# The shared-key attention stage of a two-layer decoder: float32 matmuls as three products of float32r high and low parts, and weight loads placed in other stages

## The chip, the cores and the metric

The kernel runs on one core of a Trainium2 chip. The metric is the device time of one execution in microseconds, as the median over runs. The core has TensorE (PE, matmuls, writes PSUM only), VectorE (DVE), ScalarE (ACT), GpSimd (POOL, no access to PSUM) and SyncE (SP, which here only issues DMAs). Each engine works through its own instruction stream in order and waits for the others by semaphores.

## The reference

The reference is a decoder of two layers on x of 2 batches x 512 tokens x 256 channels, each layer a mixer, a cross attention over 1,024 context rows, and a block of experts. The part that the change touches is the mixer of the second layer, an attention whose eight query heads share one key and one value projection:

```python
def _L1_attn_ref(x, proj_q, proj_k, proj_v, proj_o):
    Q = jnp.einsum('bnd,hdk->bhnk', x, proj_q)
    K = jnp.einsum('bmd,dk->bmk', x, proj_k)
    V = jnp.einsum('bmd,dv->bmv', x, proj_v)
    logits = jnp.einsum('bhnk,bmk->bhnm', Q, K)
    weights = jax.nn.softmax(logits, axis=-1)
    O = jnp.einsum('bhnm,bmv->bhnv', weights, V)
    Y = jnp.einsum('bhnv,hdv->bnd', O, proj_o)
    return Y
x = x + _L1_attn_ref(_layernorm(x, axis=-1), ...)
```

Heads have 128 columns. Behind this mixer come a cross attention that picks, for each query, the best context row ("hard cross"), and the second block of experts (256 to 1,024 channels, eight experts).

## The kernel before, in words

The program runs six stages one after the other: `mamba_stage`, `cross_stage`, `experts0_stage`, `shared_kv_stage`, `hard_cross_stage`, `experts1_stage`. Each is a block in which every engine has its own instruction list, and the engines meet between blocks.

**The stage of the change, `shared_kv_stage` (from line 1768).** A unit is one head of one batch: 16 units, batch by batch. Inside, one pipeline step (a "round" g) belongs to a tile of 128 queries, so a unit is four rounds, and there are 64 tiles. The stage has this course:
- Start: PE runs five bf16 products without use (L121), transposes the normalised input into PSUM (L112, 16 transposes), ACT copies that to `XT` (L1317). PE makes K (L1938) and V (L1947), ACT and DVE copy them out (L1901, L1847), and PE waits for these copies and for the weights `wq` and `wo`.
- The loop on PE, in this order in each round g = 4n + qt: `scores(g)` (L1970, 128 x 512); in rounds with qt 0 or 1 half of the next unit's `query_part` (L1959); `transposes(g - 3)`, four of 128 x 128 (L1978); one of four products of `output` (unit n - 1 where qt is 3, else unit n - 2) (L1988); one of four of `project` (unit n - 3) (L2000, 256 columns). Two PSUM banks each serve scores and transposes by turns.
- The other engines in a round: DVE takes the maximum of each row of scores (L1854), negates it (L1856), and makes the inverse of the sum of the round before (L1863); ACT makes the exponential with its sum (L1922); POOL multiplies by the inverse sum (L1835), 1.57 us each; DVE copies the transposes to `PT` (L1870); ACT copies the queries (L1907) and the output (L1913), each once per unit.
- DVE's order in a round: first the copy of the transposes g - 4, then the maximum of g, then the inverse sum of g - 1.
- `output(n, 0)`, the first output product of unit n, waits until all four sets of transposes of the unit are copied, which is in round 4n + 7.
- End: DVE adds the result to `X` (L1878) and `FirstQueries` (L2093, L2099) begins the next stage's queries.

**Weights.** SP loads `wq` and `wo` (1 MB each) at the start of this stage, and behind them the eight weight blocks of the second experts (L170, 1 MB each) into `area`, a buffer of 16,384 words per partition that the first experts' weights had used. `wk` and `wv` are loaded in the first experts' stage. The second experts' PE waits for all eight (`weights.loaded`).

**The hard cross stage.** It has eight units. SP's list waits for the end of an earlier unit, loads the constant rows (`tails`) and copies the query rows of unit u in parts (L2185, 64 KB each), four units ahead at most.

Of the kernel before, what the change touches and what calls it, by code (L numbers as in the profile page):

```python
# [8 lines left out]
F32 = mybir.dt.float32  # L9
BF16 = mybir.dt.bfloat16  # L10
# [4 lines left out]
P = 128  # L15
B, S, D = 2, 512, 256
T = B * S
# [1750 lines left out]
def shared_kv_stage(nc, ctx, sh, A):  # L1768
# [25 lines left out]
    def sem(name):  # L1794
# [3 lines left out]
    nm = Norm(nc, ctx, sh, "s_n")  # L1798
    nm.xn_loaded = sh.xn_back
    following = NextStatistics(sh, sem)  # L1800
    wq, wo = sb("wq", [P, H, KD, DK]), sb("wo", [P, H, D])
    wk, wv = sh.wk, sh.wv
    KTr, V = sb("KT", [P, T]), sb("V", [P, NT, DK])
    QT = [sb(f"QT{n}", [P, S]) for n in range(2)]
# [7 lines left out]
    wq_in, wo_in = sem("wq_in"), sem("wo_in")  # L1812
    kv_mm, k_ready, v_ready = sem("kv_mm"), sem("k_ready"), sem("v_ready")
    q_mm, q_ready = sem("q_mm"), sem("q_ready")
    s_mm, mx_ready, nmx_ready, p_ready, rs_ready, pn_ready, t_mm, pt_ready = (
        sem(n) for n in ("s_mm", "mx_ready", "nmx_ready", "p_ready", "rs_ready", "pn_ready", "t_mm", "pt_ready"))
    o_mm, o_ready, y_mm, y_taken = sem("o_mm"), sem("o_ready"), sem("y_mm"), sem("y_taken")

    with stage, nc.Block() as block:

        @block.sync
        def _(sp):
            sp.dma_start(wq[:, :, :, :], A["s_wq"]).then_inc(wq_in, 16)
            sp.dma_start(wo[:, :, :], A["s_wo"]).then_inc(wo_in, 16)
            queries.load(sp)
            for e in range(ExpertWeights.EXP):
                sh.weights[1].load_expert(sp, e)

        @block.gpsimd
        def _(pool):  # L1830
            for g in range(G):
# [10 lines left out]
        def _(dve):  # L1842
            for b in range(B):
                for i in range(0, TB, 2):
                    n = B + (b * TB + i) // 2
                    dve.wait_ge(kv_mm, n + 1)
                    dve.tensor_copy(V[:, b * TB + i:b * TB + i + 2, :],  # L1847
                                    PS[:, 4 + n % 4, 0:2 * DK].rearrange("p (i c) -> p i c", i=2)).then_inc(v_ready, 1)
# [16 lines left out]
            def take_transposes(g):  # L1865
                n, qt = divmod(g, TB)
                dve.wait_ge(t_mm, g + 1)
                if n >= 2:
                    dve.wait_ge(o_mm, n - 1)
                dve.tensor_copy(PT[n % 2][:, :, qt * P:(qt + 1) * P],  # L1870
                                PS[:, 2 + g % 2, :].rearrange("p (m q) -> p m q", m=TB)).then_inc(pt_ready, 1)
# [21 lines left out]
            queries.vector(dve, following.rstd_ready, nm.xT_done)  # L1893
# [3 lines left out]
        def _(act):  # L1897
            nm.scalar(act)
            for b in range(B):
                act.wait_ge(kv_mm, b + 1)  # L1900
                act.activation(KTr[:, b * S:(b + 1) * S], PS[:, 4 + b, :], ACT.Copy).then_inc(k_ready, 1)  # L1901

            def take_q(n):
                act.wait_ge(q_mm, n + 1)
                if n >= 2:
                    act.wait_ge(s_mm, (n - 1) * TB)
                act.activation(QT[n % 2][:, :], PS[:, 4, :], ACT.Copy).then_inc(q_ready, 1)  # L1907

            def take_o(n):
# [3 lines left out]
                act.activation(OT[n % 2][:, :], PS[:, 5, :], ACT.Copy).then_inc(o_ready, 1)  # L1913
# [18 lines left out]
        def _(pe):  # L1932
            spare_matmuls(pe, sh, 7, 5)
            nm.tensor(pe)
            for b in range(B):
                pe.wait_ge(nm.xT_ready, KD * (b + 1))
                for k in range(KD):
                    last = pe.matmul(PS[:, 4 + b, :], wk[:, k, :], XT[:, k, b * S:(b + 1) * S],  # L1938
                                     start=(k == 0), stop=(k == KD - 1))
                last.then_inc(kv_mm, 1)  # L1940
            for i in range(0, NT, 2):
                n = B + i // 2
                if n >= 4:
                    pe.wait_ge(k_ready, n - 3)
                for j in range(2):
                    for k in range(KD):
                        last = pe.matmul(PS[:, 4 + n % 4, j * DK:(j + 1) * DK], XT[:, k, (i + j) * P:(i + j + 1) * P],  # L1947
                                         wv[:, k, :], start=(k == 0), stop=(k == KD - 1))
                last.then_inc(kv_mm, 1)
            pe.wait_ge(k_ready, B)  # L1950
            pe.wait_ge(v_ready, NT // 2)
            pe.wait_ge(wq_in, 16)
            pe.wait_ge(wo_in, 16)

            def query_part(n, k):
                b, h = divmod(n, H)
                if n >= 1 and k == 0:
                    pe.wait_ge(q_ready, n)
                last = pe.matmul(PS[:, 4, :], wq[:, h, k, :], XT[:, k, b * S:(b + 1) * S],  # L1959
                                 start=(k == 0), stop=(k == KD - 1))  # L1960
# [3 lines left out]
            def scores(g):  # L1964
# [5 lines left out]
                pe.matmul(PS[:, g % 2, :], QT[n % 2][:, qt * P:(qt + 1) * P], KTr[:, b * S:(b + 1) * S],  # L1970
# [1414 lines left out]
```

## Time and profile before

| | us |
|---|---|
| median of 3 runs | 1010.96 |
| lowest, highest | 1007.08, 1012.14 |
| span of the profiled execution (first to last instruction) | 1003.7 |
| first experts' stage, from about 390 | to 498.5 |
| shared-key stage, start to first query | 498.5 to 509.2 |
| its loop | 509.2 to 704.9 |
| hard cross stage | 711.4 to 881 |
| second experts' stage | 881 to the end |

The profiled execution is one more execution than the three timed ones; no time beside its span is given for it, so it has to be set against the median. In the profile, PE is a matmul, PEld a weight load beside it. A record such as "560.83 1.02 PE L1970 MATMUL ... x2" is two matmul records of line 1970 that start at 560.83 us; ends of matmuls are modelled and overlap the next start, so that the time that PE spends is read from start to start. A float32 matmul has two records. "[0.99 <-PE PS L1970]" is idle time of the engine ahead of the instruction and what ended it. PEclk is the granted clock of PE as a share of 2.4 GHz.

### The profile page before, as it was taken

Reading aid. Unit: us, or ns where it says so; the run is one execution under the profiler, and the core shown is the slowest. Engines: PE = TensorE matmul, PEld = TensorE weight load, DVE = VectorE, ACT = ScalarE, POOL = GpSimd, SP = SyncE. Lnnn points to the kernel's source line nnn. Section 1 sums busy time; section 2 is a strip of 40 time slices with the busy share of each in tenths; the row PEclk is TensorE's granted clock in tenths of the full one; section 3 lists DMA queues with packets and bytes.
Section 4 is the critical chain, followed back from the end, with each engine's and each line's share of the span. In section 5 each row is a group of like instructions: output and inputs, shape, how many; then the busy total and the mean of one; then the engine's idle time right before and its main releaser. Section 6 shows DMA issues by size and latency. Waiting matters only on the chain. (4 is left out here: it accounts for less than half of the span.)

```text
span 1003.7 us, 12848 instructions
## 1 busy us (share of the span) xinstructions
PE 915.3 (91%) x4110; PEld 459.1 (46%) x4110; DVE 642.4 (64%) x1323; ACT 468.3 (47%) x928; POOL 322.9 (32%) x328
## 2 busy tenths in 40 slices
PE   5889879999999986799999999999988999859996
PEld 2445545333323235366755555555432332534565
DVE  5866558888899823455245555655689897444654
ACT  3886444677777771112133333332216777342321
POOL 7326646200000000166235545554230000115923
PEclk9999998999999997799899999999998999969999
DMA  5040036022223803633491000000200010066200
GB/s 154 1 157 0 1 61 107 1 50 49 49 50 96 289 1 112 242 105 116 144 394 40 1 0 1 1 1 1 65 17 2 32 33 1 1 246 200 75 17 27
DMA packets 41654, 73.79 MB, mean 74 GB/s; under 512 B 8964, under 2 KB 27780, under 8 KB 40436
## 3 DMA queue, kind: packets, MB, share of 16 engines
q1 hardware_dynamic: 36372, 59.68, 19.4%
q0 software_dynamic: 4400, 13.11, 4.1%
q8 instruction: 35, 0.57, 0.2%
q10 hardware_dynamic: 816, 0.17, 0.1%
q14 instruction: 31, 0.25, 0.1%
HBM read 49.67 MB, written 10.49 MB: 60 GB/s over the span
## 5 line engine op out<-in xcount | busy, mean ns | idle before, releaser
L1080 DVE TENSOR_REDUCE c_amx<-PS 128x1 f32<-128x512 f32 x256 | 159.1, 682 | 27.4 <-PE PS L980 27.1
L1173 ACT ACTIVATE c_aE<-PS 128x512 f32<-128x512 f32 x256 | 132.5, 602 | 47.1 <-PE PS L992 46.9
L1835 POOL TENSOR_SCALAR s_Pn<-s_Pr,s_rs 128x512 f32<-128x512 f32 x64 | 100.1, 1566 | 101.5 <-DVE s_rs L1863 101.2
L71 POOL TENSOR_SCALAR rstd<-mv 128x4 f32<-128x4 f32 x8 | 1.9, 233 | 335.5 <-DVE mv L94 335.5
L980 PE MATMUL PS<-c_aKs,c_aQs 99*128 99x512 bf16 x256 | 96.4, 387 | 5.1 <-DMA c_aQs<-area 3.6
L1922 ACT ACTIVATE s_Pr<-PS,s_nmx 128x512 f32<-128x512 f32 x64 | 44.0, 688 | 116.2 <-DVE s_nmx L1856 116.2
L992 PE MATMUL PS<-c_aQs,c_aKs 99*128 99x512 bf16 x256 | 94.5, 380 | 3.5 <-ACT c_aE L1173 2.3
L1854 DVE TENSOR_REDUCE s_mx<-PS 128x1 f32<-128x512 f32 x64 | 44.3, 691 | 68.7 <-PE PS L1970 68.7
L1080 DVE TENSOR_REDUCE h_amx<-PS 128x1 f32<-128x512 f32 x128 | 79.6, 682 | 8.8 <-PE PS L980 8.5
L1173 ACT ACTIVATE h_aE<-PS 128x512 f32<-128x512 f32 x128 | 67.7, 600 | 21.8 <-PE PS L992 21.4
L1003 PE MATMUL PS<-c_aE,c_VB 128*17 128x512 f32 x512 | 67.4, 598 | 0.1
L1970 PE MATMUL PS<-s_KT,s_QT 128*128 128x512 f32 x128 | 65.6, 594 | 1.0 <-ACT s_QT L1907 0.7
L1988 PE MATMUL PS<-s_PT,s_V 128*128 128x512 f32 x128 | 65.7, 595 | 0.3 <-ACT s_OT L1913 0.3
L980 PEld LDWEIGHTS PS<-c_aKs,c_aQs 99*128 99x128 bf16 x256 | 24.9, 98 | 79.0 <-DVE c_amx L1080 55.4
L3179 PE MATMUL PS<-area,g_XsT 128*128 x120 | 56.7, 617 | 0.5 <-ACT g_XsT L3116 0.5
L980 PE MATMUL PS<-h_aKs,h_aQs 99*128 99x512 bf16 x128 | 49.8, 397 | 7.7 <-DVE h_amx L1080 7.1
L1870 DVE COPY s_PT<-PS 128x512 f32<-128x512 f32 x64 | 44.2, 690 | 10.9 <-PE PS L1978 10.9
L992 PE MATMUL PS<-h_aQs,h_aKs 99*128 99x512 bf16 x128 | 48.7, 392 | 2.1 <-ACT h_aE L1173 1.2
L1978 PEld LDWEIGHTS PS<-ident,s_Pn 128*128 128x128 f32 x256 | 31.9, 141 | 32.5 <-issue 26.1
L3121 ACT ACTIVATE g_H<-g_H 128x1024 f32<-128x1024 f32 x15 | 15.9, 1058 | 53.0 <-DVE g_H L3055 53.0
L992 PEld LDWEIGHTS PS<-c_aQs,c_aKs 99*128 99x128 bf16 x256 | 24.6, 98 | 32.2 <-ACT c_aE L1173 9.6
L1978 PE MATMUL PS<-ident,s_Pn 128*128 128x128 f32 x256 | 38.4, 273 | 0.0
(440 smaller groups left out, 1696.8 us busy)
## 6 DMA issues: line engine op xcount, KB each, us to landing
area<-in_e_w SPq DMA_DIRECT2D x16, 512.0 KB, 9.5
area<-in_g_w SPq DMA_DIRECT2D x8, 1024.0 KB, 17.1
c_aKs<-area SPq DMA_DIRECT2D x48, 128.0 KB
g_B<-in_g_b SPq DMA_DIRECT2D x1, 4096.0 KB, 14.3
c_aQs<-area SPq DMA_DIRECT2D x48, 64.0 KB
h_aQs<-h_QP SPq DMA_DIRECT2D x48, 64.0 KB
early<-in_ctxT SPq DMA_DIRECT2D x2, 1024.0 KB, 8.6
e_B<-in_e_b SPq DMA_DIRECT2D x1, 2048.0 KB
```

What stands on the lines that cost most here:

```text
L980: pe.matmul(PS[:, n % MB, :], self.Qs[u % self.NQ][:, j, qt * P:(qt + 1) * P], self.Ks[self.key_buffer(u)][:, j % self.KH, half * BANK:(ha ...
L992: pe.matmul(PS[:, MB + n % XB, :], self.Ks[self.key_buffer(u)][:, j % self.KH, kt * P:(kt + 1) * P], self.Qs[u % self.NQ][:, j, :], start= ...
L1003: last = pe.matmul(PS[32 * j:32 * j + VW, 6, :], self.V[:, self.value_unit(u), kt, j % self.KH, :], self.E[kt % 2][:, j, :], start=(kt == ...
L1080: dve.tensor_reduce(self.mx[:, qt, j, half:half + 1], PS[:, n % MB, :], AX.X, ALU.max).then_inc(self.max_done, 1)
L1173: act.activation(self.E[kt % 2][:, j, :], PS[:, MB + x % XB, :], ACT.Exp, scale=0.25).then_inc(self.exp_done, 1)
L1835: pool.tensor_scalar(Pn[g % NPB][:, :], Pr[g % NPB][:, :], rs[:, g % NPB:g % NPB + 1], None, ALU.mult).then_inc(pn_ready, 1)
L1854: dve.tensor_reduce(mx[:, g % NPB:g % NPB + 1], PS[:, g % 2, :], AX.X, ALU.max).then_inc(mx_ready, 1)
L1870: dve.tensor_copy(PT[n % 2][:, :, qt * P:(qt + 1) * P], PS[:, 2 + g % 2, :].rearrange("p (m q) -> p m q", m=TB)).then_inc(pt_ready, 1)
L1970: pe.matmul(PS[:, g % 2, :], QT[n % 2][:, qt * P:(qt + 1) * P], KTr[:, b * S:(b + 1) * S], start=True, stop=True).then_inc(s_mm, 1)
L1978: last = pe.transpose(PS[:, 2 + g % 2, m * P:(m + 1) * P], Pn[g % NPB][:, m * P:(m + 1) * P], sh.ident[:, :])
L1988: last = pe.matmul(PS[:, 5, :], V[:, n // H * TB + m, :], PT[n % 2][:, m, :], start=(m == 0), stop=(m == TB - 1))
L3179: last = pe.matmul(PS[:, 1 + p % 2 * NB1 + half, :], XsT[p % 2][:, k, :], W1[:, k, bass.ds(e * F + half * BANK, BANK)], start=(k == 0), st ...
```

## The change

Each operand of the stage's matmuls is split into a high part, which is the value written as float32r, and a low part, the value less the high part, also written as float32r. Each product f x m becomes f_high x m_high + f_high x m_low + f_low x m_high, accumulated in PSUM. Transposes stay as they are. High parts are written by ACT (for `wk`, `wv`, `wo` by DVE), low parts by DVE (for `wq` by POOL). The copy of the transposes moves from DVE to ACT, and each low part is a new DVE instruction, in the rounds as the diff shows. The tiles `PT` and the split `wq` and `wo` take all of `area`; so `wq` and `wo` are loaded in the first experts' stage, into buffers of their own, and the second experts' weights in the hard cross stage, two behind the query rows of each of the units 4 to 7.

The diff, without the declarations of semaphores and the comments of context:

```diff
@@ shared_kv_stage
-    PT = [sb(f"PT{n}", [P, TB, S]) for n in range(2)]
-    OT = [sb(f"OT{n}", [P, S]) for n in range(2)]
+    PT = [[overlaid(f"PT{part}{n}", [P, TB, S]) for part in "hl"] for n in range(2)]
+    wqs, wos = ([overlaid(f"{name}{part}", shape) for part in "hl"]
+                for name, shape in (("wq", [P, H, KD, DK]), ("wo", [P, H, D])))
+    XTs, KTs, Vs = split("XT", [P, KD, T]), split("KT", [P, T]), split("V", [P, NT, DK])
+    wks, wvs = split("wk", [P, KD, DK]), split("wv", [P, KD, DK])
+    QT, OT = ([split(f"{name}{n}", [P, S]) for n in range(2)] for name in ("QT", "OT"))
...
         def _(sp):
-            sp.dma_start(wq[:, :, :, :], A["s_wq"]).then_inc(wq_in, 16)
-            sp.dma_start(wo[:, :, :], A["s_wo"]).then_inc(wo_in, 16)
             queries.load(sp)
-            for e in range(ExpertWeights.EXP):
-                sh.weights[1].load_expert(sp, e)
...
         def _(pool):
+            pool.wait_ge(wqh_ready, 1)
+            pool.tensor_tensor(wqs[1][:, :, :, :], wq[:, :, :, :], wqs[0][:, :, :, :].bitcast(F32),
+                               ALU.subtract).then_inc(wq_ready, 1)
...
         def _(dve):
+            for w, parts in ((wk, wks), (wv, wvs)):
+                dve.tensor_copy(parts[0][:, :, :], w[:, :, :]).then_inc(wh_ready, 1)
+            dve.tensor_copy(wos[0][:, :, :], wo[:, :, :]).then_inc(wh_ready, 1)
+            dve.wait_ge(wh_ready, 2)
+            for w, parts in ((wk, wks), (wv, wvs)):
+                dve.tensor_tensor(parts[1][:, :, :], w[:, :, :], parts[0][:, :, :].bitcast(F32),
+                                  ALU.subtract).then_inc(w_ready, 1)
+            dve.wait_ge(wh_ready, 3)
+            dve.tensor_tensor(wos[1][:, :, :], wo[:, :, :], wos[0][:, :, :].bitcast(F32),
+                              ALU.subtract).then_inc(w_ready, 1)
+            for g in range(KD * B):
+                b, k = divmod(g, KD)
+                cols = slice(b * S, (b + 1) * S)
+                dve.wait_ge(xkvh_ready, g + 1)
+                dve.tensor_tensor(XTs[1][:, k, cols], PS[:, g, :], XTs[0][:, k, cols].bitcast(F32),
+                                  ALU.subtract).then_inc(xkv_ready, 1)
+            for n in range(NKV):
+                high, low = kv_parts(n)
+                dve.wait_ge(xkvh_ready, KD * B + n + 1)
+                dve.tensor_tensor(low, kv_bank(n), high.bitcast(F32), ALU.subtract).then_inc(xkv_ready, 1)
...
+            def low_queries(n):
+                dve.wait_ge(qh_ready, n + 1)
+                dve.tensor_tensor(QT[n % 2][1][:, :], PS[:, 4, :], QT[n % 2][0][:, :].bitcast(F32),
+                                  ALU.subtract).then_inc(q_ready, 1)
+
+            def low_output(n):
+                dve.wait_ge(oh_ready, n + 1)
+                dve.tensor_tensor(OT[n % 2][1][:, :], PS[:, 5, :], OT[n % 2][0][:, :].bitcast(F32),
+                                  ALU.subtract).then_inc(o_ready, 1)
...
+                dve.wait_ge(pth_ready, g + 1)
+                dve.tensor_tensor(PT[n % 2][1][:, :, cols], PS[:, 2 + g % 2, :].rearrange("p (m q) -> p m q", m=TB),
+                                  PT[n % 2][0][:, :, cols].bitcast(F32), ALU.subtract).then_inc(pt_ready, 1)
...
-            for g in range(G + LAG + 1):
-                if g > LAG:
-                    take_transposes(g - LAG - 1)
+            low_queries(0)
+            for g in range(STEPS):
+                n, qt = divmod(g, TB)
+                v, m = output_part(g - 1)
+                if 0 <= v < UN and m == TB - 1:
+                    low_output(v)
                 if g < G:
                     maximum(g)
                 if 1 <= g <= G:
                     inverse_sum(g - 1)
+                if 0 <= g - LAG - 1 < G:
+                    low_transposes(g - LAG - 1)
+                if qt == 2 and n + 1 < UN:
+                    low_queries(n + 1)
...
         def _(act):
-            nm.scalar(act)
+            act.activation(wqs[0][:, :, :, :], wq[:, :, :, :], ACT.Copy).then_inc(wqh_ready, 1)
+            for g in range(KD * B):
+                b, k = divmod(g, KD)
+                act.wait_ge(xT_done, g + 1)
+                act.activation(XTs[0][:, k, b * S:(b + 1) * S], PS[:, g, :], ACT.Copy).then_inc(xkvh_ready, 1)
+            for n in range(NKV):
+                act.wait_ge(kv_mm, n + 1)
+                act.activation(kv_parts(n)[0], kv_bank(n), ACT.Copy).then_inc(xkvh_ready, 1)
...
             for g in range(STEPS):
                 n, qt = divmod(g, TB)
+                if 0 <= g - LAG - 1 < G:
+                    take_transposes(g - LAG - 1)
...
         def _(pe):
+            def products(out, fixed, moving, start, stop):
+                for i, (f, m) in enumerate(((0, 0), (0, 1), (1, 0))):
+                    last = pe.matmul(out, fixed[f], moving[m], start=(start and i == 0), stop=(stop and i == 2),
+                                     skip_group_check=True)
+                return last
...
+            pe.wait_ge(w_ready, 2)
             for b in range(B):
-                pe.wait_ge(nm.xT_ready, KD * (b + 1))
+                pe.wait_ge(xkv_ready, KD * (b + 1))
...
-            pe.wait_ge(k_ready, B)
-            pe.wait_ge(v_ready, NT // 2)
-            pe.wait_ge(wq_in, 16)
-            pe.wait_ge(wo_in, 16)
+            pe.wait_ge(xkv_ready, KD * B + NKV)
+            pe.wait_ge(wq_ready, 1)
+            pe.wait_ge(w_ready, 3)
...
-                last = pe.matmul(PS[:, 4, :], wq[:, h, k, :], XT[:, k, b * S:(b + 1) * S],
-                                 start=(k == 0), stop=(k == KD - 1))
+                last = products(PS[:, 4, :], [w[:, h, k, :] for w in wqs], [x[:, k, b * S:(b + 1) * S] for x in XTs],
+                                k == 0, k == KD - 1)
...
@@ hard_cross_stage, SP
                     query_part(u, p)
+                if u >= NQ:
+                    for e in range(2 * (u - NQ), 2 * (u - NQ + 1)):
+                        sh.weights[1].load_expert(sp, e)
@@ experts0_stage
+    sh.wq = sh.held.enter_context(nc.sbuf_tensor("s_wq", [P, EXPERTS, KD, P], F32))
+    sh.wo = sh.held.enter_context(nc.sbuf_tensor("s_wo", [P, EXPERTS, D], F32))
...
+            sp.dma_start(sh.wq[:, :, :, :], A["s_wq"]).then_inc(wkv_in, 16)
+            sp.dma_start(sh.wo[:, :, :], A["s_wo"]).then_inc(wkv_in, 16)
...
-            sp.wait_ge(wkv_in, 32)
+            sp.wait_ge(wkv_in, 64)
```

K, V, scores, outputs and projections are changed in the same way as the queries shown.

## Rows read from the trace of the kernel before

**Rows 1.** The profile's page, busy time (us, share of the span, instructions)
```profile
PE 915.3 (91%) x4110; PEld 459.1 (46%) x4110; DVE 642.4 (64%) x1323; ACT 468.3 (47%) x928; POOL 322.9 (32%) x328
```

**Rows 2.** Windows of two stretches: us, busy of each engine, PEclk, DMA share, GB/s
```profile
509.20:704.90 195.70, 194.26 (x704) 109.76 (x705) 105.74 (x270) 65.77 (x160) 101.33 (x66) 1.00 0.11 43
711.40:881.00 169.60, 153.14 (x750) 58.83 (x750) 133.34 (x269) 90.70 (x169) 17.89 (x21) 0.98 0.07 22
```

**Rows 3.** Timeline of PE in one round of the loop: start, us, engine, line
```profile
560.40 0.59 PE L2000 MATMUL PS<-s_wo,s_OT 128*128 128x256 f32 x2
560.83 1.02 PE L1970 MATMUL PS<-s_KT,s_QT 128*128 128x512 f32 x2
561.69 1.02 PE L1959 MATMUL PS<-XT,s_wq 128*128 128x512 f32 x2
562.55 0.60 PE L1978 MATMUL PS<-ident,s_Pn 128*128 128x128 f32 x4
562.99 1.02 PE L1988 MATMUL PS<-s_PT,s_V 128*128 128x512 f32 x2
```

**Rows 4.** Timeline of the other engines in the same round and the next
```profile
561.89 0.69 DVE L1854 TENSOR_REDUCE s_mx<-PS 128x1 f32<-128x512 f32 x1 [0.99 <-PE PS L1970]
562.62 0.15 DVE L1856 TENSOR_SCALAR s_nmx<-s_mx 128x1 f32<-128x1 f32 x1
562.70 0.16 DVE L1863 RECIPROCAL s_rs<-s_sm 128x1 f32<-128x1 f32 x1
562.81 0.69 ACT L1922 ACTIVATE s_Pr<-PS,s_nmx 128x512 f32<-128x512 f32 x1 [1.81 <-DVE s_nmx L1856]
562.95 1.57 POOL L1835 TENSOR_SCALAR s_Pn<-s_Pr,s_rs 128x512 f32<-128x512 f32 x1 [1.02 <-DVE s_rs L1863]
563.19 0.69 DVE L1870 COPY s_PT<-PS 128x512 f32<-128x512 f32 x1 [0.33 <-PE PS L1978]
566.25 0.69 ACT L1922 ACTIVATE s_Pr<-PS,s_nmx 128x512 f32<-128x512 f32 x1 [2.67 <-DVE s_nmx L1856]
566.93 0.59 ACT L1907 ACTIVATE s_QT<-PS 128x512 f32<-128x512 f32 x1
```

**Rows 5.** Groups by line and form, DVE: busy us, mean ns | idle before
```profile
L1878 DVE TENSOR_TENSOR X<-X,PS 128x512 f32<-128x512 f32 x4 | 2.6, 684 | 8.2 <-PE PS L2000 8.2
```

**Rows 6.** Timeline of the start of the stage, PE and DVE
```profile
498.58 1.24 PE L121 MATMUL PS<-identb 128*128 128x512 bf16 x5 [0.30 <-PEq L2543]
499.65 1.91 PE L112 MATMUL PS<-ident,X 128*128 128x128 f32 x16
501.43 3.70 PE L1938 MATMUL PS<-XT,s_wk 128*128 128x512 f32 x8
504.96 3.73 PE L1947 MATMUL PS<-s_wv,XT 128*128 128x128 f32 x32
508.74 0.42 DVE L1847 COPY s_V<-PS 128x256 f32<-128x256 f32 x1 [0.47 <-PE PS L1947]
509.26 1.96 PE L1959 MATMUL PS<-XT,s_wq 128*128 128x512 f32 x4 [0.56 <-DVE s_V L1847]
```

**Rows 7.** Groups by line and form, operations of 2,048 elements
```profile
L500 DVE TENSOR_TENSOR m_base<-m_base,X 128x2048 f32<-128x2048 f32 x1 | 2.3, 2291 | 0.1
L341 POOL TENSOR_TENSOR m_base<-m_base,X 128x2048 f32<-128x2048 f32 x1 | 4.7, 4697 | 0.1
```

**Rows 8.** Pauses of PE (timeline) and the granted clock behind them (windows)
```profile
63.68 0.37 PE L815 MATMUL PS<-area,m_DL 56*128 56x512 bf16 x1 [3.48 <-ACT area L689]
...
63.60:68.00 4.40, 4.32 (x11) 1.52 (x11) 2.95 (x4) 3.17 (x8) 4.25 (x3) 0.61 0.98 342
...
900.25 0.51 PE L3169 MATMUL PS<-ident,g_Xs 128*128 128x128 f32 x2 [2.58 <-DMA g_Xs<-g_xn_rows,g_inv_src]
...
900.00:908.00 8.00, 6.46 (x11) 2.76 (x12) 1.38 (x8) 2.05 (x3) 2.83 (x3) 0.57 0.88 281
```

**Rows 9.** DMA issues: kind, count, KB each, median us to landing
```profile
area<-in_g_w SPq DMA_DIRECT2D x8, 1024.0 KB, 17.1
```

More of the change, by code:

```diff
@@ L9 @@
 F32 = mybir.dt.float32
+F32R = mybir.dt.float32r
 BF16 = mybir.dt.bfloat16
@@ L1906, in take_q @@
                     act.wait_ge(s_mm, (n - 1) * TB)
[L1907 removed]
+                act.activation(QT[n % 2][0][:, :], PS[:, 4, :], ACT.Copy).then_inc(qh_ready, 1)
             def take_o(n):
@@ L1912, in take_o, with take_transposes @@
                     act.wait_ge(y_mm, n - 1)
-                act.activation(OT[n % 2][:, :], PS[:, 5, :], ACT.Copy).then_inc(o_ready, 1)
+                act.activation(OT[n % 2][0][:, :], PS[:, 5, :], ACT.Copy).then_inc(oh_ready, 1)
+            def take_transposes(g):
+                n, qt = divmod(g, TB)
+                act.wait_ge(t_mm, g + 1)
+                if n >= 2:
+                    act.wait_ge(o_mm, n - 1)
+                act.activation(PT[n % 2][0][:, :, qt * P:(qt + 1) * P],
+                               PS[:, 2 + g % 2, :].rearrange("p (m q) -> p m q", m=TB), ACT.Copy).then_inc(pth_ready, 1)
             take_q(0)
@@ L1943, in _ @@
                 if n >= 4:
-                    pe.wait_ge(k_ready, n - 3)
+                    pe.wait_ge(xkv_ready, KD * B + n - 3)
                 for j in range(2):
                     for k in range(KD):
-                        last = pe.matmul(PS[:, 4 + n % 4, j * DK:(j + 1) * DK], XT[:, k, (i + j) * P:(i + j + 1) * P],
-                                         wv[:, k, :], start=(k == 0), stop=(k == KD - 1))
+                        last = products(PS[:, 4 + n % 4, j * DK:(j + 1) * DK],
+                                        [x[:, k, (i + j) * P:(i + j + 1) * P] for x in XTs], [w[:, k, :] for w in wvs],
+                                        k == 0, k == KD - 1)
                 last.then_inc(kv_mm, 1)
-            pe.wait_ge(k_ready, B)
-            pe.wait_ge(v_ready, NT // 2)
-            pe.wait_ge(wq_in, 16)
-            pe.wait_ge(wo_in, 16)
+            pe.wait_ge(xkv_ready, KD * B + NKV)
+            pe.wait_ge(wq_ready, 1)
+            pe.wait_ge(w_ready, 3)
             def query_part(n, k):
@@ L1969, in scores @@
                     pe.wait_ge(p_ready, g - 1)
-                pe.matmul(PS[:, g % 2, :], QT[n % 2][:, qt * P:(qt + 1) * P], KTr[:, b * S:(b + 1) * S],
-                          start=True, stop=True).then_inc(s_mm, 1)
+                products(PS[:, g % 2, :], [q[:, qt * P:(qt + 1) * P] for q in QT[n % 2]],
+                         [x[:, b * S:(b + 1) * S] for x in KTs], True, True).then_inc(s_mm, 1)
             def transposes(g):
@@ L1987, in output @@
                         pe.wait_ge(o_ready, n)
-                last = pe.matmul(PS[:, 5, :], V[:, n // H * TB + m, :], PT[n % 2][:, m, :], start=(m == 0),
-                                 stop=(m == TB - 1))
+                last = products(PS[:, 5, :], [v[:, n // H * TB + m, :] for v in Vs], [p[:, m, :] for p in PT[n % 2]],
+                                m == 0, m == TB - 1)
                 if m == TB - 1:
@@ L1999, in project @@
                         pe.wait_ge(y_taken, 2 * b)
-                last = pe.matmul(PS[:, 6 + i // 2, (i % 2) * D:(i % 2 + 1) * D], OT[n % 2][:, i * P:(i + 1) * P],
-                                 wo[:, h, :], start=(h == 0 and i % 2 == 0), stop=(h == H - 1 and i % 2 == 1),
-                                 skip_group_check=True)
+                last = products(PS[:, 6 + i // 2, (i % 2) * D:(i % 2 + 1) * D],
+                                [o[:, i * P:(i + 1) * P] for o in OT[n % 2]], [w[:, h, :] for w in wos],
+                                h == 0 and i % 2 == 0, h == H - 1 and i % 2 == 1)
                 if i == TB - 1:
```

65 lines of the change are left out of this document (34 added, 31 removed).

## The prediction

> **What bounds the kernel now.** I read the views in this order. The totals [rows 1] show TensorE (PE) busy for 91% of the span; that is a sum over six stages, so I cut the span by stage. In the loop of the shared-key stage, the upper of the two stretches of [rows 2], PE is busy 194.26 of 195.70 us at full clock while VectorE (DVE) has 105.74, ScalarE (ACT) 65.77 and GpSimd (POOL) 101.33: in this stretch nothing but PE sets the time. The records of one round [rows 3] give the prices, from start to start: a float32 product of 512 columns 0.86 us (560.83 to 561.69), a projection of 256 columns 0.43, four transposes 0.44. A unit (one head of one batch) is four rounds with ten products of 512 columns (4 scores, 2 query, 4 output), four projections and four sets of transposes: 8.6 + 1.72 + 1.76 = 12.08 us, and 16 units make 193 us, which is the loop. The other engines' records of the same round [rows 4] show what hangs on what: the maximum starts 0.20 after PE has passed the scores, its result leaves after 0.73, the negated maximum reaches ACT 0.19 later, the exponential holds ACT 0.68 (566.25 to 566.93), and the inverse sum takes 0.08 to 0.10 of DVE. At present all of this lies beside PE.
>
> **PE's own work after the change.** Each float32 product becomes three float32r products. No float32r record is in the trace. The lower bound of one with 512 columns is the bf16 product, 0.215 us (five spare ones from 498.58 to 499.65 [rows 6]); the upper bound is one of the two records that a float32 product has, 0.43. I take 0.216: high times high, high times low and low times high are three of the four products of halves that the 0.86 us seem to hold, so one should cost a quarter of it. The Trainium skill ("FP8 and Floating Point Precision", TensorE Precision Notes) says that true FP32 takes four passes and that reduced precision only truncates what it reads; by it, too, three passes stand against four. Weight loads do not go below 0.11 us (four transposes in 0.44 [rows 3]), which is about the stream of 256 columns; so 0.65 for 512 columns, 0.33 for 256. PE's work in a unit is then 10 x 0.65 + 4 x 0.33 + 1.76 = 9.58 us in place of 12.08. If PE still set the pace the loop would save 16 x 2.5 = 40 us.
>
> **Why I do not count that.** The change puts three new steps on DVE (low parts of transposes, queries, outputs) and moves the copy of the transposes to ACT. A low part reads PSUM and SBUF and writes 128x512, like the addition of 0.684 us [rows 5]. DVE's work per unit becomes 4 x (0.73 + 0.18 + 0.64) + 2 x 0.64 = 7.5 us, ACT's 4 x (0.68 + 0.5) + 2 x 0.5 = 5.7, POOL's 4 x 1.57 = 6.3: none is the bound by its sum. The order is. In round 4n+7 PE's first output product of unit n waits for the low part of transposes 4n+3. DVE does that part behind the low part of output n-1, the maximum of scores 4n+7 and an inverse sum; before, the copy stood ahead of the maximum. Walk one unit from the moment that PE starts output(n, 0) in round 4n+7:
> - PE runs without a stop through output, projection; scores, query, transposes, output, projection; the same five again; scores 4n+10: 8 x 0.65 + 3 x 0.33 + 2 x 0.44 = 7.07 us.
> - Scores to maximum 0.20, maximum 0.73, to ACT 0.19, exponential 0.68: 8.87. Only then ACT, in order, copies the output of unit n (o_mm came at 8.36): 0.59 and 0.06 to DVE [rows 4]: 9.52. DVE has meanwhile done its low transposes and low queries, until 9.46.
> - Low output 0.64, maximum 0.73, negation and inverse 0.18, low transposes 0.69 and 0.15 until PE has reloaded weights: 11.91.
> There output(n+1, 0) starts. PE has 9.58 us of work in these 11.91 and pauses 2.33 us once per unit. The unit takes 11.9 in place of 12.08: about 2 us less over the loop. The last units have longer ends, since each hand-over is now two steps (ACT, then DVE, 0.69 more at q, PT and o, each once at the ends): 2 us more. Loop: 0, with 0.3 us per unit (5 us) either way for hand-overs that I read from one round. If the low part's SBUF read ran against POOL's, it would take more than 0.69 (twice per chain): inside those 5 us.
>
> **The clock, a term of its own.** PE now pauses. The trace shows what pauses do: after one of 3.48 us the granted clock of 63.6 to 68 is 0.61, which is 4.4 x 0.39 = 1.7 us of full-speed work lost at 1.2 GHz; after one of 2.58 us (900.25) it is 0.57 over 8 us, 3.4 us lost [rows 8]. My pause of 2.33 us is a little shorter than the second. I take it that seven of the 15 pauses lower the clock for a stretch like the first, since PE's part of the chain (7.07 us) follows right behind the pause and stretches with it: 7 x 1.7 = 12 us. Bounds: none, and 15 x 3.4 = 51.
>
> **The start of the stage.** Now the transposes end and K begins at 501.43, V at 504.96, and the first query at 509.26 [rows 6]. After the change DVE starts at about 498.55 with the high parts: wk and wv 0.4 each, like the copy of V [rows 6], wo (2,048 elements) at most the 2.29 us of an addition of that size [rows 7], I take 2.2; low parts of wk and wv 0.8, of wo 2.3: until 504.6. Only then come the four low parts of XT, 0.64 each. K of batch 0 waits for two of them, 505.95, and PE has been idle 4.5 us. K takes 12 products of 0.216: 508.7. V is 16 x 3 products of 128 columns at the load floor 0.11, 5.3 us: 514.0 (0.22 each, as two of today's records, would add 5). The last bank goes through ACT (0.4) and DVE (0.42) in 1.2 us: the queries start at 515.25, 6.0 us later than now. The Trainium skill ("VectorE: DVE Perf Modes", Mode 2x_2P) says that an fp32 copy within SBUF moves two elements per cycle; by it the copy of wo would be 1.1 us shorter and the stage would start so much earlier. No wide copy of this kind is in the trace. The idle 4.5 us are longer than either pause of [rows 8], so K and V begin at 1.2 GHz: 1.7 to 3.4 us less whatever waits for DVE anyway, taken as 2. Hidden: ACT's high part of wq (2,048 elements, four times 0.59 at most) ends before the transposes do; POOL's low part of wq costs 4.7 us [rows 7] and ends at about 506, 9 us before it is needed; if POOL were half as fast that cover would still hold.
>
> **The moved loads.** The eight expert weights (1 MB each, 17.1 us to landing at the median [rows 9]) leave this stage's queue and go to the hard cross stage, two behind each of the last four units' query rows. That stage is 169.6 us long [rows 2] for eight units; the last pair is issued once unit 3 is done, some 70 us before its end, and the query rows queued behind a pair are wanted three units later. SP gets 2.8 us more of issuing in a unit of some 18. Cost 0. wq and wo (2 MB) move into the first experts' stage behind the context; a gather queued beside them is asked for three tiles ahead. Cost 0, at most 2. The barriers stay. At the end of the loop DVE normalises four tiles only after the last low output, 1.6 us beside 1.3 us of projections: 0.4.
>
> **Sum.** +6.0 + 2.0 + 0 + 12 + 0.4 = +20.4 us. The profiled span is 1003.7 and the median of the runs 1010.96, so about 7 us lie around the span and stay. Forecast 1031.
>
> **Rivals.** (A) The forecast: chain and falling clock, 0.45, own range 1023 to 1048. (B) The chain, but the clock holds through pauses of 2.33 us: 1019, 0.22; for it, the pause is shorter than both that lowered the clock. (C) A float32r product costs more than a quarter of a float32 one. At 0.43 for 512 columns the chain's PE part is 8 x 1.29 + 3 x 0.65 + 0.88 = 13.2, the unit 18 us and the time 1114; if the type changes nothing and each of the three costs 0.86, the change does not do what it says and the unit is 30 us (8 x 2.58 + 3 x 1.29 + 0.88 + 4.84) and the time about 1300. Together 0.12, since the spare products show 0.215 only for bf16. (D) Faster: the queue on DVE does not bind. The wait of output(n, 0) would be met when PE arrives, 2.33 us earlier than in my walk; then PE's work rules, 1011 - 40 + 8 = 979. It decides from a unit of 11.2 us on, 0.9 under 12.08, which pays the 8 us of the start and 5 more. 0.11; against it stands that the order of DVE's steps is fixed in the code. (E) The chain is 0.5 us shorter than my sum and the clock holds: 16 x 0.5 = 8 us back, 1011, 0.10.
> A measurement of this kernel can tell 0.5% (5 us) from no change. Faster 0.11 (D), same 0.12 (E and the low edge of B), slower 0.77. The range 1008 to 1052 holds A, B and most of E.
>
> **What would show it.** Right: scores, queries and outputs as three records of about 0.22 us; one PE idle of about 2.3 us per unit, ended by DVE's low transposes; a unit of 12 us with PE near 80% busy; granted clock under 1.00 in the loop; queries starting 16 to 18 us into the stage. Wrong: records of 0.43; a unit of 9.6 us; DVE's low parts far from 0.69; PE waiting in the hard cross stage for query rows, or in the experts' stages for weights or gathers.

## The result, and the profile after

The changed kernel takes 1039.87 us (median of four executions, 1039.53 to 1041.43). The kernel before, beside it, takes 1009.02 (1005.81 to 1012.14): a ratio of 1.0321, 95% interval 1.0294 to 1.0348, so 3.2% slower. The forecast was 1031, with a range of 1008 to 1052.

The span of the profiled execution went from 1003.7 to 1039.6 us. Windows of the changed kernel, of the loop (to its last projection), the start of the stage, K, the hard cross stage, and two stretches inside the loop; the columns are those of [rows 2], PEclk the third from the end:

```profile
519.30:741.70 222.40, 189.88 (x926) 154.51 (x927) 121.06 (x302) 97.79 (x224) 101.34 (x66) 0.89 0.00 1
498.00:519.30 21.30, 13.42 (x82) 11.28 (x82) 14.28 (x16) 6.68 (x11) 4.67 (x1) 0.83 0.36 101
508.15:512.89 4.74, 4.74 (x12) 3.74 (x13) 1.74 (x3) 0.60 (x1) 0.00 (x0) 0.57 0.00 0
748.40:919.75 171.35, 153.00 (x753) 58.94 (x754) 133.98 (x273) 90.55 (x169) 18.14 (x23) 0.98 0.21 73
605.00:607.00 2.00, 2.00 (x8) 1.61 (x7) 0.25 (x1) 0.00 (x0) 0.00 (x0) 0.50 0.00 0
658.90:671.90 13.00, 10.62 (x58) 8.58 (x58) 10.14 (x28) 6.03 (x16) 6.22 (x5) 1.00 0.01 3
```

Set beside the trace of before, the 35.9 us come from these places. First stages -0.6. Start of the stage (first spare product to first query) 10.68 to 21.30: +10.6. Loop (first query to the next stage's first transpose, 509.26 to 705.03 before, 519.30 to 741.94 after) 195.8 to 222.6: +26.9. From there to the hard cross stage 6.48 and 6.48. Hard cross stage (PE's first product of it to the first transpose of the second experts, 711.51 to 882.62 before, 748.42 to 919.06 after; the window above ends 0.7 us later) 171.1 to 170.6, second experts 121.1 to 120.6. These stages moved by half a microsecond each; what changed lies in the shared-key stage.

**Inside the loop.** PE's waits in the changed kernel (waited for: us in total, times, longest), and PE's records of one unit with the rounds in the middle left out:

```profile
PE PS L2005 <- DVE s_PTl L1919: 28.9, 16, 2.1
PE PS L2005 <- DVE s_QT0l L1907: 1.4, 1, 1.4
```

```profile
603.71 0.50 PE L2005 MATMUL PS<-s_PTh,s_Vh 128*128 128x512 f32 x1 [1.83 <-DVE s_PTl L1919]
604.04 0.40 PE L2005 MATMUL PS<-s_PTl,s_Vh 128*128 128x512 f32 x1
604.28 0.51 PE L2005 MATMUL PS<-s_PTh,s_Vl 128*128 128x512 f32 x1
...
605.23 0.63 PE L2005 MATMUL PS<-s_KTh,s_QT1h 128*128 128x512 f32 x1
605.66 0.63 PE L2005 MATMUL PS<-s_KTl,s_QT1h 128*128 128x512 f32 x1
606.09 0.63 PE L2005 MATMUL PS<-s_KTh,s_QT1l 128*128 128x512 f32 x1
...
612.19 0.39 PE L2005 MATMUL PS<-s_KTh,s_QT1h 128*128 128x512 f32 x1
612.42 0.39 PE L2005 MATMUL PS<-s_KTl,s_QT1h 128*128 128x512 f32 x1
612.65 0.39 PE L2005 MATMUL PS<-s_KTh,s_QT1l 128*128 128x512 f32 x1
612.88 0.60 PE L2055 MATMUL PS<-ident,s_Pn 128*128 128x128 f32 x4
...
615.07 0.60 PE L2055 MATMUL PS<-ident,s_Pn 128*128 128x128 f32 x4
617.50 0.50 PE L2005 MATMUL PS<-s_PTh,s_Vh 128*128 128x512 f32 x1 [1.83 <-DVE s_PTl L1919]
```

A float32r product of 512 columns costs 0.23 us from start to start (612.19 to 612.42), so three of them 0.70 in place of 0.86 [rows 3]. Behind the pause the same products come 0.43 apart (605.23 to 605.66): the granted clock is 0.50 there, that is 1.2 GHz. (The last of the windows is a unit without a fall; it is 13.00 us long because DVE adds the output of batch 0 to `X` in it and takes the statistics of the sum, from 660.36 to 663.42, before it gets to the next maximum.) One pause per unit, 16 in all and 13 of them 1.82 to 1.84 us long, is ended by DVE's low part of the transposes, and the unit takes 13.79 us (603.71 to 617.50). DVE and ACT in the second half of this unit:

```profile
613.08 0.69 DVE L1894 TENSOR_REDUCE s_mx<-PS 128x1 f32<-128x512 f32 x1 [1.33 <-PE PS L2005]
613.80 0.15 DVE L1896 TENSOR_SCALAR s_nmx<-s_mx 128x1 f32<-128x1 f32 x1
...
615.29 0.69 DVE L1912 TENSOR_TENSOR s_OT1l<-PS,s_OT1h 128x512 fp32r<-128x512 f32 x1
615.90 0.68 DVE L1894 TENSOR_REDUCE s_mx<-PS 128x1 f32<-128x512 f32 x1
616.62 0.15 DVE L1896 TENSOR_SCALAR s_nmx<-s_mx 128x1 f32<-128x1 f32 x1
616.70 0.16 DVE L1903 RECIPROCAL s_rs<-s_sm 128x1 f32<-128x1 f32 x1
616.78 0.67 DVE L1919 TENSOR_TENSOR s_PTl<-PS,s_PTh 128x512 fp32r<-128x512 f32 x1
```

```profile
613.99 0.69 ACT L1992 ACTIVATE s_Pr<-PS,s_nmx 128x512 f32<-128x512 f32 x1 [1.13 <-DVE s_nmx L1896]
614.58 0.19 ACT L1992 ACTIVATION_READ_ACCUMULATOR s_Pr<-PS,s_nmx 128x1 f32 x1
614.67 0.59 ACT L1973 ACTIVATE s_OT1h<-PS 128x512 fp32r<-128x512 f32 x1
```

This is the chain as it was walked: scores end 612.88, maximum 613.08, exponential 613.99, high part of the output 614.67, its low part 615.29, next maximum 615.90, low transposes 616.78, PE at 617.50. That is 4.62 us; the forecast had 4.84.

**The start of the stage**, DVE first, then POOL, then PE of the changed kernel:

```profile
498.41 1.22 DVE L1871 CAST s_woh<-s_wo 128x2048 fp32r<-128x2048 f32 x1
499.55 0.42 DVE L1874 TENSOR_TENSOR s_wkl<-s_wk,s_wkh 128x256 fp32r<-128x256 f32 x1
499.88 0.42 DVE L1874 TENSOR_TENSOR s_wvl<-s_wv,s_wvh 128x256 fp32r<-128x256 f32 x1
500.22 6.59 DVE L1877 TENSOR_TENSOR s_wol<-s_wo,s_woh 128x2048 fp32r<-128x2048 f32 x1
506.73 2.47 DVE L1883 TENSOR_TENSOR s_XTl<-PS,s_XTh 128x512 fp32r<-128x512 f32 x4
```

```profile
499.99 4.67 POOL L1855 TENSOR_TENSOR s_wql<-s_wq,s_wqh 128x2048 fp32r<-128x2048 f32 x1 [6.72 <-ACT s_wqh L1954]
```

```profile
508.15 0.77 PE L2005 MATMUL PS<-s_XTh,s_wkh 128*128 128x512 f32 x1 [6.73 <-DVE s_XTl L1883]
```

The low part of wo holds DVE 6.59 us in place of the 2.3 expected. It comes to the engine 0.23 us behind POOL's subtraction of the same size. POOL ends at 504.66, and 2.15 us later DVE is done: as if it had stood for as long as POOL worked. Experiment 5 tests this. K then waits 6.73 us, and most of K runs at a clock of 0.57.

**The moved loads.** DMA issues of the hard cross stage onwards: the median landing of the second experts' weights is 6.7 us, in place of 17.1 [rows 9], and no wait of PE names them. Experiment 6 tests what moving them does to the time.

```profile
area<-in_g_w SPq DMA_DIRECT2D x8, 1024.0 KB, 6.7
```

### The profile page after: what moved, and what is told of

It reads as the page before. It is cut to its first block and busy times, and to the rows that moved or that the text cites. A ratio compares the mean times of both kernels' runs of the same rounds, so it can differ in the third digit from the quotient of the medians.

```text
span 1039.6 us, 13450 instructions
## 1 busy us (share of the span) xinstructions
PE 915.1 (88%) x4354; PEld 506.9 (49%) x4354; DVE 669.2 (64%) x1367; ACT 503.6 (48%) x997; POOL 326.6 (31%) x329
## 5 line engine op out<-in xcount | busy, mean ns | idle before, releaser
L2005 PE MATMUL PS<-s_PTh,s_Vh 128*128 128x512 f32 x64 | 32.0, 499 | 28.9 <-DVE s_PTl L1919 28.9
L1919 DVE TENSOR_TENSOR s_PTl<-PS,s_PTh 128x512 fp32r<-128x512 f32 x64 | 43.1, 673 | 3.7 <-ACT s_PTh L1980 3.7
L2055 PE MATMUL PS<-ident,s_Pn 128*128 128x128 f32 x256 | 40.8, 284 | 1.1 <-DVE s_PTl L1919 1.1
L1980 ACT ACTIVATE s_PTh<-PS 128x512 fp32r<-128x512 f32 x64 | 38.0, 593 | 4.9 <-PE PS L2055 4.7
```

The lines of the kernel that those rows point to most:

```text
L1919: dve.tensor_tensor(PT[n % 2][1][:, :, cols], PS[:, 2 + g % 2, :].rearrange("p (m q) -> p m q", m=TB), PT[n % 2][0][:, :, cols].bitcast(F3 ...
L1980: act.activation(PT[n % 2][0][:, :, qt * P:(qt + 1) * P], PS[:, 2 + g % 2, :].rearrange("p (m q) -> p m q", m=TB), ACT.Copy).then_inc(pth_ ...
L2055: last = pe.transpose(PS[:, 2 + g % 2, m * P:(m + 1) * P], Pn[g % NPB][:, m * P:(m + 1) * P], sh.ident[:, :])
```

## The experiments

All times are medians with a ratio to executions of the kernel before on the same chip.

**1. Spare products in the pause.** The changed kernel; PE runs eight bf16 products without use once the low queries are there, ahead of each unit's first output product.

```diff
+                if 0 <= v < UN and m == 0:
+                    pe.wait_ge(q_ready, min(n + 2, UN))
+                    spare_matmuls(pe, sh, 4, 8)
                 if 0 <= v < UN:
                     output(v, m)
```

> The changed kernel with eight bf16 products without use (512 columns, about 0.216 us each, 1.7 us together) on PE in its pause of some 2.07 us per unit, ahead of the first output product of a unit. Nothing else waits for them. My theory has two parts: the hand-over chain through ACT and DVE sets the unit, and the pause it leaves on PE lowers the granted clock once per unit (0.89 over the loop of 222.6 us, so 24 us lost). Then the clock of the loop goes to 1.00 and the time falls by 20 to 24 us, from 1040 to 1016 to 1020, while the wait for the low transposes is still there once per unit, shorter by the 1.7 us that the spare products fill. Rival: the clock does not matter, since in its slow stretches PE is waiting for DVE anyway: time within 4 us of 1040, clock 1.00 all the same. Second rival: eight products in front of the output lengthen the unit: slower by up to 14 x 1.7 = 24 us.

Measured 1022.76 us, ratio 1.0143 (1.0103 to 1.0183): 17.1 us less, 2.8 above the expected 1016 to 1020. The span is 18.7 us under the changed kernel's. Its loop, and three records of it:

```profile
520.95:721.89 200.94, 195.66 (x1055) 150.02 (x1056) 121.07 (x302) 97.12 (x224) 101.35 (x66) 1.00 0.00 1
```

```profile
597.98 0.50 PE L2005 MATMUL PS<-s_PTh,s_Vh 128*128 128x512 f32 x1
...
608.23 1.89 PE L122 MATMUL PS<-identb 128*128 128x512 bf16 x8
610.23 0.50 PE L2005 MATMUL PS<-s_PTh,s_Vh 128*128 128x512 f32 x1
```

The clock holds at 1.00 and the loop, measured as above, is 21.5 us shorter (222.6 to 201.2), although PE has more to do. The unit is 12.25 us (597.98 to 610.23): the chain without the clock. So each unit of 13.8 us loses 1.55 to the clock. Not all of the 21.5 us reach the span: the stage begins 0.9 us later and its start takes 0.8 longer than in the changed kernel's profile, and neither was edited.

**2. Half as many.** The same with `spare_matmuls(pe, sh, 4, 4)`.

> The changed kernel with four spare bf16 products in the pause of each unit, in place of the eight that held the clock at 1022.76 us. They fill 0.86 of some 2 us, so PE still idles 1.0 to 1.2 us per unit. Theory (a), the clock stands a pause of 1.0 us: granted clock 1.00 in the loop, the unit 12.02 us (the chain without anything of the spares in it), the loop 197 to 198, the time 1019 to 1021. Rival (b), any pause of this size lowers the clock: loop above 215, the time 1035 to 1040.

Measured 1024.36 us, ratio 1.0143 (1.0112 to 1.0173). PE's waits of the loop, and its clock:

```profile
PE PS L2005 <- DVE s_PTl L1919: 15.0, 16, 1.2
```

```profile
523.20:724.05 200.85, 182.25 (x990) 143.77 (x991) 121.13 (x302) 97.13 (x224) 101.36 (x66) 1.00 0.00 1
```

Theory (a): with pauses of 0.97 us the clock stays whole. The loop is as long as with eight, so the unit of 12.25 us is the chain's and not the spare products'. The time is 3 us over the upper end of (a): the loop, measured as above, is 201.1 in place of 197 to 198, since the chain is 12.25 us and not the 12.02 that I expected. This execution's stage also begins 3.0 us later than the changed kernel's, at 501.04.

**3. Outputs and projections one round later.** Then the last low part of a unit's transposes has a whole round before PE asks for it.

```diff
-    STEPS = G + 2 * TB + LAG + 1
+    STEPS = G + 2 * TB + LAG + 2
...
-        v, m = divmod(g - LAG, TB)
+        v, m = divmod(g - LAG - 1, TB)
...
-        v, i = divmod(g - LAG - 1, TB)
+        v, i = divmod(g - LAG - 2, TB)
...
-                if (g - LAG - 1) % TB == TB - 1 and (g - LAG - 1) // TB - 2 == H - 1:
+                if projection_part(g) == (H - 1, TB - 1):
                     take_output(0)
```

> The changed kernel with output and projection one round later on PE (and the steps on ACT, DVE and at the batch change that follow them). All work stays; only the distance between the transposes of a unit's last tile and its first output product grows by one round of some 2.4 us. Theory (the chain of hand-overs sets the unit, not the amount of work on any engine): PE arrives later than the low transposes, the pause of 2 us per unit goes, the clock stays at 1.00, and PE's own work rules: 10 x 0.70 + 4 x 0.36 + 4 x 0.36 = 9.9 us per unit in place of 13.8, with some waits left 10.3. The loop falls from 222.6 to about 171 and the time from 1040 to about 988. Rival: DVE has become the bound by the sum of its steps (154.7 us busy of 222.6, with gaps between dependent steps): then the unit hardly moves, and the time stays above 1025. Second rival: each hand-over bank of PSUM is the limit, so the wait only moves to another line (queries or output): 1010 to 1030.

Measured 996.41 us, ratio 0.9866 (0.9823 to 0.9908): now 1.3% faster than before. The loop, the first output product of two units that follow each other, and PE's longest waits on DVE's low parts in the loop:

```profile
523.48:696.14 172.66, 165.47 (x927) 137.70 (x927) 120.90 (x302) 97.05 (x224) 101.41 (x66) 1.00 0.00 1
...
600.76 0.47 PE L2005 MATMUL PS<-s_PTh,s_Vh 128*128 128x512 f32 x1
...
610.94 0.47 PE L2005 MATMUL PS<-s_PTh,s_Vh 128*128 128x512 f32 x1
```

```profile
PE PS L2055 <- DVE s_PTl L1919: 2.1, 3, 1.3
PE PS L2005 <- DVE s_OT0l L1912: 1.9, 3, 1.1
```

The 16 waits are gone and with them the falls of the clock: the loop, measured as above, is 172.9, 49.7 us less, where about 171 was expected. The time missed 988 by 8. In the profiled execution the stage begins 3.2 us later than in the changed kernel's, its start takes 0.9 longer, the hard cross stage 0.7 and the second experts 1.3; none of this was edited. (Over these profiles the stage begins anywhere between 494.3 and 501.2.)

**4. Low transposes ahead of the maximum on DVE.** The other way to shorten the chain: no step is removed, only two are exchanged.

```diff
+                if 0 <= g - LAG - 1 < G:
+                    low_transposes(g - LAG - 1)
                 if g < G:
                     maximum(g)
                 if 1 <= g <= G:
                     inverse_sum(g - 1)
-                if 0 <= g - LAG - 1 < G:
-                    low_transposes(g - LAG - 1)
```

> The changed kernel with DVE's low part of the transposes ahead of the maximum in a round, where the copy of the transposes stood in the kernel before. If the time were lost only because the low part had been put behind the maximum, this would shorten the chain by the maximum, the negation and the inverse, 0.9 us per unit, and give 14 us back: 1026. My walk says the opposite: the low part now waits for ACT's copy, which ACT does ahead of its exponential but behind the one before, so the maximum of the round gets stuck behind that wait in every round, and with it the exponential and the next scores. I expect the same time or slower: 1040 to 1055, with DVE idle ahead of the low transposes in most rounds in place of ahead of the maximum.

Measured 1037.92 us, ratio 1.0291 (1.0250 to 1.0332), the same as the changed kernel. DVE's waits (first line) and PE's (second):

```profile
DVE s_PTl L1919 <- ACT s_PTh L1980: 65.9, 47, 1.8
```

```profile
PE PS L2005 <- DVE s_PTl L1919: 29.3, 16, 2.7
```

The maximum that stood in front is out of the way, but DVE now waits 65.9 us (3.7 in the changed kernel) for ACT's high part of the transposes, with the maximum queued behind. In most rounds the maximum starts 0.85 to 2.6 us after the start of the last product of its scores, in the changed kernel 0.43 to 1.06; the exponential starts later with it, and so do ACT's high parts. A unit without a fall of the clock is 12.33 us (604.72 to 617.05) against 12.25. The penalty that was expected (1040 to 1055) did not come, and no clear gain either: the wait moved from one place of the ring to another. The loop of the profiled execution is 217.4 us, 5.3 less than the changed kernel's, at a granted clock of 0.92, because the clock fell behind fewer of the pauses. Here are the 4 us behind two of them, of 1.89 and 1.91 us:

```profile
604.72:608.72 4.00, 4.00 (x22) 3.41 (x23) 2.31 (x7) 1.69 (x4) 1.84 (x2) 1.00 0.02 4
617.05:621.05 4.00, 4.00 (x14) 3.17 (x15) 2.37 (x7) 1.64 (x4) 1.79 (x2) 0.64 0.00 0
```

**5. GpSimd's subtraction of wq behind DVE's weight steps.**

```diff
             pool.wait_ge(wqh_ready, 1)
+            pool.wait_ge(w_ready, 3)
```

> The changed kernel with one wait added: POOL's subtraction of the high part of wq starts only when DVE has done its subtraction for wo. In the trace of the changed kernel the two run at the same time, 4.67 us on POOL and 6.59 us on DVE, where DVE needed 2.29 us for an addition of that size before. Theory: the two collide in reading or writing SBUF. Then DVE's takes about 2.3 us, the low parts of XT start 4.3 us earlier, PE idles 2.4 us in place of 6.7 before K, and the time falls by 4 to 7 us (the upper end if the clock also holds), to 1033 to 1036. POOL's part ends near 507.5, long before the queries need it. Rival: writing float32r makes the instruction slow by itself: DVE's still takes 6.6 us, nothing moves, 1040.

Measured 1036.88 us (1028.5 to 1040.87), ratio 1.0298 (1.0255 to 1.0341), 1 us over the expected 1033 to 1036. DVE and PE at the start:

```profile
496.51 2.28 DVE L1878 TENSOR_TENSOR s_wol<-s_wo,s_woh 128x2048 fp32r<-128x2048 f32 x1
```

```profile
500.14 0.47 PE L2006 MATMUL PS<-s_XTh,s_wkh 128*128 128x512 f32 x1 [2.38 <-DVE s_XTl L1884]
```

The low part of wo is back at 2.28 us, K's wait goes from 6.73 to 2.38 us, K runs at full clock, and the start takes 15.07 us in place of 21.30: 6.2 less. Of this only 3 us arrive in the median, and as the ratios' intervals overlap, a gain in the whole time is not shown by this run. Its five executions spread over 12 us, and their mean granted clocks go with them: 0.951 in the fastest, which is the profiled one, 0.937 in the slowest. In which stretch the slower ones lost it is not shown; the loop of the profiled one still takes 219.1 us at 0.91.

**6. The moved loads alone.** The kernel before with its two groups of loads placed as in the change; all products float32.

> The kernel before, with the moved loads of the change alone: the weights of the shared-key stage loaded in the first experts' stage, those of the second experts in the hard cross stage; every product stays float32. My prediction gave these loads nothing, at most 2 us. Theory (a): 1009, within 5 us, the hard cross and the experts' stages as long as before within 0.5 us, the loop of the shared-key stage 193 us. Rival (b): the loads hide a loss or a gain that the trace of the changed kernel gives to something else (contention with the gathers or query rows): over 5 us either way.

Measured 1008.03 us (12 executions) beside 1008.35 (17): ratio 0.9997 (0.9978 to 1.0017), and a loop of 195.8 us as before. The loads neither cost nor give anything that shows, within 2 us.

**7 to 9. A version that beats both.** The edits of experiments 3 and 5 together, first without spare products (experiment 7):

> The same as the one before it without the spare products: outputs and projections one round later and GpSimd's subtraction of wq behind VectorE's weight steps. Theory: the PE idle ahead of K is 2.4 us as with GpSimd's wait alone, the clock there mostly holds, and the time is 990, within 2 us of the version with spare products. Rival: the clock falls at K although the idle is 2.4 us, which costs 2 to 4 us and lets the version with spare products win by as much.

989.64 us, ratio 0.9811 (0.9797 to 0.9826), in the middle of the expectation. In one point the theory failed: the wait ahead of K is 2.86 us and not 2.4, and the clock falls there (0.90 over the start), as the rival had it; the first query comes 16.67 us into the stage. The same with eight spare products behind the transposes, ahead of K (experiment 8):

```diff
+            spare_matmuls(pe, sh, 7, 8)
             pe.wait_ge(w_ready, 2)
```

> The changed kernel with outputs and projections one round later, GpSimd's subtraction of wq behind VectorE's weight steps, and eight spare bf16 products of 512 columns ahead of K. Theory: the gains add up, since they lie in different stretches: 996.4 of the later outputs, less about 6 us of the stage's start: 990, the span's first query 15 to 16 us into the stage at full clock, the loop 172.7 at granted clock 1.00. Rival (a): the earlier start is partly given back, as PE then meets the loop's first steps before the subtraction of wq: 993 to 996. Rival (b): the spare products keep K at full clock but make K wait themselves, so no gain over the same without them.

988.49 us, ratio 0.9801 (0.9785 to 0.9817). The first query comes 15.1 us into the stage (498.87 to 513.96) at clock 1.00, 1.6 earlier than without; K's own start, 5.85 us in, is the same. By the ratios the two versions can't be told apart. Last, in place of the spare products, DVE's two steps of wo behind the low parts of XT (experiment 9):

```diff
-            dve.tensor_copy(wos[0][:, :, :], wo[:, :, :]).then_inc(wh_ready, 1)
...
-            dve.tensor_tensor(wos[1][:, :, :], wo[:, :, :], wos[0][:, :, :].bitcast(F32),
-                              ALU.subtract).then_inc(w_ready, 1)
             for g in range(KD * B):
...
+            dve.tensor_copy(wos[0][:, :, :], wo[:, :, :]).then_inc(wh_ready, 1)
+            dve.wait_ge(wh_ready, 3)
+            dve.tensor_tensor(wos[1][:, :, :], wo[:, :, :], wos[0][:, :, :].bitcast(F32),
+                              ALU.subtract).then_inc(w_ready, 1)
```

> Outputs and projections one round later and GpSimd's wait, as in the version without spare products (989.64 us), and VectorE now splits wo behind the low parts of XT, no longer ahead of them. wo takes 1.2 us for the copy and 2.3 for the low part, and K waits for neither, only for two low parts of XT. Theory: K begins about 3 us into the stage in place of 5.85, at full clock, since the idle ahead of it is under 1 us; K and V take 8.1 us and the first query comes 12.6 us into the stage in place of 16.7: 4 us less, 985.6. Rival: the low parts of K now come behind wo's 3.5 us, and GpSimd's subtraction of wq behind them too, so that the first query waits for one of the two: no gain.

987.45 us, ratio 0.9785 (0.9758 to 0.9812). K begins 3.84 us into the stage in place of 5.85, the first query comes at 13.18 in place of 16.67: 3.5 of the 4 us expected. K is not at 3 since ACT splits wq (1.9 us) before it gets to XT. The median is 2.2 us lower than without this edit, but the intervals of the two ratios overlap, so that the gain shows in the trace and not in the times. Against the kernel before it is 2.1% faster. PE's wait ahead of K and the loop:

```profile
504.59 0.47 PE L2006 MATMUL PS<-s_XTh,s_wkh 128*128 128x512 f32 x1 [0.86 <-DVE s_XTl L1880]
```

```profile
513.93:686.47 172.54, 165.32 (x927) 137.63 (x927) 120.88 (x302) 97.16 (x224) 101.47 (x66) 1.00 0.00 1
```

## Why the prediction was right, and what it mis-sized

The mechanism and the sign were right (rival A): PE's work falls, a chain over DVE and ACT takes its place, PE pauses once per unit, and the clock falls. Experiments 1 and 3 show the two parts apart: spare products take away the fall of the clock alone, one more round takes away the wait as well. The time lies 9 us above the forecast and inside the range.

That it lies so near is in part luck. Over the two profiles the terms are: start +10.6 (forecast 8), loop without the clock +5.4 (0), clock +21.5 (12), end of the stage 0 (0.4), the other stages -1.6 (0), together +35.9 and not +20.4. Added to the median of 1010.96 from which I started they would give 1047; the median of the changed kernel is 1039.87, mostly because the profile of before was one of the fastest executions. By steps:

- **Price of a product.** 0.216 forecast, 0.232 measured. Transposes went from 0.44 to 0.36 for four (experiment 3, 600.40 to 600.76), which I had left at 0.44; that is 0.09 us each, so the 0.11 that I had taken as the least time of a weight load was no floor. Rival C (0.43 and more) is out: 0.43 appears only where the clock is 0.50.
- **The chain.** 11.91 forecast, 12.25 measured: PE's part is 7.63 (597.98 to 605.61 with spare products) and not 7.07, since products are dearer, the first product behind transposes takes 0.32 and not 0.23, and projections are 3 x 0.12; the part over DVE and ACT is 4.62 and not 4.84. Over 16 units +2.7 us against before in place of -2. The ends of the loop gave the rest of +5.4 (195.8 to 201.2): 2.7, where 2 was forecast.
- **The clock in the loop, the term that was furthest off.** I let seven of 15 pauses lower the clock, 12 us. The number seven followed from no row. Thirteen of the 16 units show a stretch at half clock; experiment 1 gives 21.5 us back. The price of one, 1.7, was near (1.55): the count was off. Rivals B and E, in which the clock holds, are out by PEclk 0.89.
- **The start.** +8 forecast (6 and 2 for the clock), +10.6 measured. The copy of wo was cheaper (1.22, not 2.2), its low part much dearer (6.59, not 2.3); V came out as said (5.3 us). The low part of wo was priced from a row in which nothing ran on POOL [rows 7], in a stage in which I had just put a POOL subtraction beside it.
- **The copy of wo and the rule on it.** 2,048 elements in 1.22 us, of which the trace of before had no row. By the Trainium skill ("VectorE: DVE Perf Modes", Mode 2x_2P) an fp32 copy within SBUF moves two elements per cycle, and the trace agrees.
- **The end of the stage.** +0.4 forecast, 0 measured (6.48 both). The moved loads: 0 forecast, shown by experiment 6.
- **What lies around the span.** I added 7 us (1010.96 less 1003.7). The changed kernel's profiled execution took 1041.43 around a span of 1039.6: it is 1.8 us. A span of 1003.7 then belongs to one of the fastest executions of before (the lowest is 1005.81), and the rest of the 7 was scatter. The terms measured add up to 35.9 over that profile; between medians it is 30.9.
- **Rival D** (the queue on DVE does not bind) is out: the 16 waits are there. What it would have given shows in experiment 3, where the queue no longer binds: the loop falls by 23 us under before and not by 40. A unit of pure PE work is 10.18 us there (600.76 to 610.94, from one output product behind transposes and query to the same one a unit later), not 9.58; 16 of them are 163 us, and the other 10 of the 172.9 are the fill and drain of the longer pipeline and a few short waits.

## What to carry to other kernels

When an edit makes the bounding engine's work smaller, walk the ring of hand-overs once around in the order written in each engine's list. The pace is set by the longer of the two, PE's work or the walk. A small shortfall can cost twice, since PE's pause can lower the granted clock for what follows; one more round of distance between producer and consumer (experiment 3) took away wait and clock loss together, while exchanging two steps on the busy engine moved nothing. Price an operation with the neighbour that it will have, not from a row where it ran alone.

## What the runs showed of the hardware

- In the changed kernel's loop the granted clock fell to 0.50 (1.2 GHz) behind 13 of the 14 pauses of 1.82 to 2.09 us, and not behind the two of 1.34 and 1.66. Pauses of 0.97 us in the same places (experiment 2) left it at 1.00. One of 2.38 us ahead of K (experiment 5) did too, while one of 2.86 us there lowered it (experiment 7, clock 0.90); each of these two was seen once.
- The length of a pause alone does not tell: of seven pauses of 1.89 to 1.92 us in experiment 4, three were followed by a clock of 0.58 to 0.64 over the next 4 us, and four by 1.00. What decides between them stays open here. I had rows of 2.58 and 3.48 us to go by [rows 8], and no pause that the clock had stood.
- A DVE subtraction of two SBUF tensors stands still while a POOL subtraction runs: 6.59 us beside it, 2.28 without; POOL's own went from 4.67 to 4.60 only. By the Trainium skill ("SBUF — State Buffer", Who interferes with whom) the two engines share a port pair as an exclusive lock, and an operation with two SBUF inputs that comes second is blocked until the first is through; the trace agrees in length and in order. The low parts of the loop's transposes, with one input in PSUM, were not held up: 61 of 64 ran beside a POOL instruction, in 0.67 us, the other three in 0.69.
- The projection, 256 columns, costs 0.12 us per float32r product, V's products of 128 columns 0.11, and one of 512 columns 0.23: 128 columns cost nearly as much as 256.
